# Attention with a softmax that is kept unnormalised for one of eight query blocks, on one core

## What is computed

```python
x  = L0_attn_x                                   # [8, 1024, 512]
xn = layernorm(x)
q, k, v = xn @ Wq.T, xn @ Wk.T, xn @ Wv.T        # 16 heads of 32
attn = softmax(q k^T * 512**-0.5)                # [b, h, s, t]
attn = attn + bias_table[s - t + 1023]           # added after the softmax; the index is clipped at 1022
s = layernorm(attn v) * ln_gamma + ln_beta
h = square(relu(xn @ W_fc.T)); y = h @ W_proj.T  # 2048 hidden
g = silu(mean over 5 steps of the spikes of a leaky integrator driven by y)
return x + s * g
```

## Time and profile before

| | |
|---|---|
| median of three runs | 3528.83 us (3526.05 to 3529.1) |
| span of the profiled execution | 3528.6 us; the page gives no time outside the span |
| feed-forward part, 0 to 1330 us | PE busy 1307.08 us |
| 1500 to 3400 us | PE busy 1856.82 us, ACT 1887.48, DVE 1548.66, POOL 1311.54 of 1900 |
| granted TensorE clock | 1.00 in that stretch, that is 2.4 GHz |

### The profile page before, as it was taken

One profiled execution on the slowest core, in us unless ns is written; L12 is line 12 of the kernel. 1 busy time (PEld: TensorE's weight loads), 2 busy tenths in 40 slices (PEclk: granted clock), 3 DMA queues, 4 the chain that ended last, 5 costly groups with the idle time before them and its releaser, 6 DMA issues.

```text
span 3528.6 us, 55344 instructions
## 1 busy us (share of the span) xinstructions
PE 3421.4 (97%) x19961; PEld 1441.3 (41%) x19964; DVE 2506.6 (71%) x4051; ACT 2624.2 (74%) x3898; POOL 1720.5 (49%) x998
## 2 busy tenths in 40 slices
PE   7999999999999999999999999999999999999996
PEld 3444444444444444433433433433433433433431
DVE  5555555555555555777888888888888888888887
ACT  6433333333333335999999999999999999999997
POOL 0012222111111123899666666666666666666672
PEclk9999999999999999999999999999999999999999
DMA  5122322333222222222322322322322322322322
GB/s 186 57 80 80 104 79 80 101 96 103 80 79 79 81 83 86 83 67 72 121 88 84 95 87 83 96 87 84 96 85 83 98 85 82 100 85 82 100 61 84
DMA packets 238752, 312.35 MB, mean 89 GB/s; under 512 B 96624, under 2 KB 132208, under 8 KB 238480
## 3 DMA queue, kind: packets, MB, share of 16 engines
q1 hardware_dynamic: 238480, 308.82, 28.2%
HBM read 174.65 MB, written 76.61 MB: 71 GB/s over the span
## 4 chain that ended last, share of the span: by engine, by line
ACT 33%; PE 11%; issue 10%; DVE 4%; SPq 1%; DMA 1%; ACTq 0%; POOL 0%; DVEq 0%; POOLq 0%
ACT recurrence_or_probs L1457 17%; ACT s_sb L1464 16%; PE misc L1331 3%; PE acc L1406 3%; PE s_ps L1386 3%; PE s_ps L1372 2%; DVE s_sb L1533 2%; DMA xT<-xnT 1%; SPq L322 1%; DVE gate_or_tokens L1662 0%; PE misc L1313 0%; DVE outT L1553 0%; DVE x_or_queries L1570 0%; DVE gate_or_tokens L1665 0%; PE s_ps L1331 0%
## 5 line engine op out<-in xcount | busy, mean ns | idle before, releaser
L1739 POOL TENSOR_TENSOR recurrence_or_probs<-recurrence_or_probs,toep 128x512 f32<-128x512 f32 (+1 forms) x375 | 1288.5, 3457 | 366.5 <-ACT recurrence_or_probs L1457 366.2
L1533 DVE TENSOR_SCALAR_CACHE_REDUCE s_sb<-s_ps 128x1024 f32<-128x1024 f32 x998 | 1213.7, 1220 | 353.8 <-PE s_ps L1372 325.7
L1464 ACT ACTIVATE s_sb<-s_sb,nmax 128x1024 f32<-128x1024 f32 x998 | 1167.0, 1169 | 9.8 <-DVE s_sb L1533 9.5
L1457 ACT ACTIVATE recurrence_or_probs<-s_ps 128x1024 f32<-128x1024 f32 x1024 | 1060.1, 1036 | 7.7 <-PE s_ps L1386 7.5
L559 PE MATMUL ps_fc<-xnT_part,w_fc 128*128 128x512 f16 x3072 | 707.2, 380 | 4.5 <-DVE w_fc L817 4.5
L574 PE MATMUL ps_y<-w_pr,hid_part 128*128 128x512 f16 x3072 | 706.2, 380 | 3.6 <-issue 2.6
L740 ACT ACTIVATE relu<-ps_fc 128x512 f32<-128x512 f32 x256 | 152.7, 597 | 626.9 <-PE ps_fc L559 626.9
L130 POOL TENSOR_TENSOR recurrence_or_probs<-gate_or_tokens,beta_row 128x512 f32<-128x512 f32 x60 | 89.9, 1499 | 1035.3 <-DVE gate_or_tokens L185 1031.7
L929 DVE TENSOR_TENSOR hid<-relu 128x512 f32<-128x512 f32 x256 | 210.3, 822 | 510.9 <-ACT relu L740 510.9
L1406 PE MATMUL acc<-recurrence_or_probs,val 128*32 128x512 f32 x4096 | 545.2, 604 | 2.2 <-DVE recurrence_or_probs L1649 1.5
L559 PEld LDWEIGHTS ps_fc<-xnT_part,w_fc 128*128 128x128 f16 x3072 | 300.6, 98 | 369.3 <-issue 7.8
(11 more groups left out here) (180 smaller groups left out, 2685.1 us busy)
## 6 DMA issues: line engine op xcount, KB each, us to landing
toep<-table_rows SPq DMA_DIRECT2D x32, 2048.0 KB, 8.3
x_or_queries<-x_or_queries SPq DMA_DIRECT2D x384, 64.0 KB, 2.0
x_or_queries<-in_x SPq DMA_DIRECT2D x16, 1024.0 KB, 10.4
xnT<-xnT_part SPq DMA_DIRECT2D x32, 512.0 KB, 8.5
x_or_gate<-in_x SPq DMA_DIRECT2D x16, 1024.0 KB, 9.2
base<-x_or_gate SPq DMA_DIRECT2D x16, 1024.0 KB, 6.8
xT<-xnT SPq DMA_DIRECT2D x32, 512.0 KB, 9.7
result<-gate_or_tokens SPq DMA_DIRECT2D x64, 256.0 KB, 2.0
```

Source lines behind the costliest of these rows:

```text
L1457: nc.scalar.activation(prob[:, k % PROBS, 2 * second:2 * second + 2, :].rearrange("p j n -> p (j n)"), s_ps[:, item_buffer(pair_item(m)), ...
L1464: nc.scalar.activation(s_sb[:, i % 4, :], s_sb[:, i % 4, :], ACT.Exp, bias=nmax[:, par, j, st:st + 1], scale=-1.0, accum_out=den[:, par, j ...
L1533: nc.vector.tensor_scalar(s_sb[:, i % 4, :], s_ps[:, item_buffer(tile_item(n)), :], -1.0, None, ALU.mult, ALU.min, accum_out=nmax[:, par, ...
L1739: nc.gpsimd.tensor_tensor(tile, tile, toep[:, par, :, at:at + width], ALU.add).then_inc(biased, 1)
```

## The change

Six things change in attention.

1. **The last query block** (`LATE = 7`, queries 896 to 1023) is no longer normalised before the exponential. Its four tiles of a group still give their row maximum (by `tensor_reduce`, with no copy), but `exp_sum` skips them; the logarithm that is subtracted for them stays 0. The order of the tiles (`TILE_ORDER`) puts them at half steps 12, 21, 27 and 2. `s_sb` has three buffers instead of four.
2. **Its denominators**: POOL adds the eight key blocks' exponentials of those 128 queries (`sum_late`, seven additions of 128x512), PE sums them over the keys with a matrix of ones (`late_denominators`, half step 3 of the next slot), and DVE takes the reciprocal and multiplies the output by it.
3. **The bias**: the table now holds differences from its last row, which is zero for the constant part; the constant part is added as the sum of all values of the batch times that row, from sums of tokens that DVE takes in the feed-forward part (`sum_tokens`, two in each chunk) and one set of 48 products in slot 0. `sum_values` of every slot goes. For the last query block PE weighs the bias with the values (`late_bias`, half step 8), and POOL's additions for it go.
4. **The order of the keys** is `KEY_ORDER`, so that wide and narrow additions on POOL alternate.
5. **Weighings come in twos**, in the second half step of every odd step: those of k-3 and k-2.
6. **The projections** are placed anew: the values at half steps 0, 1, 5 and 6, each projection of queries or keys in three parts of four products instead of two of six, and the hand-over of the subtracted rows one half step later.

In the prologue the table is loaded and stored back before the second set of weights is loaded; in the last slot the gate's last tiles are loaded into `xT`.

```diff
+TILE_ORDER = ((0, 0), (0, 1), (0, 2), (0, 3), (1, 0), (1, 1), (0, 7), (1, 2), (1, 3), (2, 0), (2, 1), (2, 2), (2, 3), (3, 0), (3, 1), (1, 7),
...
+LATE = 7
...
-VALUES = {0: (0, 0), 2: (0, 1), 4: (1, 0), 6: (1, 1)}
...
-SUM_VALUES, ROWS_1, ROWS_0, OUT_1, OUT_0 = 8, 10, 27, 28, 30
+VALUES = {0: (0, 0), 1: (0, 1), 5: (1, 0), 6: (1, 1)}
+QUERY_KEYS = {12 + 4 * u + i: (u, i) for u in range(4) for i in range(3)}
+QK_PARTS = 3
+LATE_BIAS = 8
+FAR_VALUES, ROWS_1, ROWS_0, OUT_1, OUT_0 = 4, 10, 28, 29, 30
+KEY_ORDER = ((4, 0, 5, 1, 6, 2, 7, 3), (0, 4, 1, 5, 2, 3, 6, 7))
+COPY_1, COPY_0 = 4, 20
...
+        def weighed_at(b, hg, k):
+
+            ready = (k - WEIGH_LAG, k - WEIGH_LAG + 1) if k % 2 else ()
+            return [(b, hg, i) if i >= 0 else (*before(b, hg), SLOT_STEPS + i) for i in ready]
...
+            def late_denominators(g):
+
+                take_misc()
+                pe.wait_ge(biased, pool_count(g, SLOT_STEPS - 1))
+                pe.wait_ge(ones_made, 1)
+                for j in range(HG):
+                    last = nc.tensor.matmul(misc[j * HD:(j + 1) * HD, :P], ones_col[:], late_sum[:, j, :], start=True, stop=True)
...
+            def late_bias(s):
+
+                take_misc()
+                pe.wait_ge(v_read, s.g * 2 + 2)
+                pe.wait_ge(toep_loaded[s.par], toep_uses(s.b, s.hg) * 16)
+                for j in range(HG):
+                    last = nc.tensor.matmul(misc[j * HD:(j + 1) * HD, :P], val[:, s.par, LATE, j * HD:(j + 1) * HD],
+                                            toep[:, s.par, j, TW - P:], start=True, stop=True)
...
             def exp_sum(G, par, i):
                 n = G * 32 + i
-                j, st = i % 16 // 4, i // 16 * 4 + i % 4
+                j, st = TILE_ORDER[i]
+                if not SUMMED[i]:
+                    return
+                copy = summed_before(n) % COPIES
...
+                if not SUMMED[i]:
+                    nc.vector.tensor_reduce(nmax[:, par, j, st:st + 1], s_ps[:, item_buffer(tile_item(n)), :], AX, ALU.max,
+                                            negate=True).then_inc(max_done, 1)
+                    return
...
+                nc.vector.reciprocal(late_scale[:], misc[:, :P]).then_inc(den_read, 1)
+                nc.vector.tensor_scalar(outT[:, 1, :late.start], acc[:, :late.start], from_far, None, ALU.add)
+                dve.wait_ge(den_read, g + 1)
+                nc.vector.tensor_tensor(outT[:, 1, late], acc[:, late], late_scale[:], ALU.mult).then_inc(acc_read, 1)
+                dve.wait_ge(acc_read, g * 2 + 2)
+                nc.vector.tensor_tensor(outT[:, 1, late], outT[:, 1, late], late_out[:], ALU.add).then_inc(out_made, 1)
...
+            def sum_late(b, hg, k):
+
+                g, late = b * HG + hg, slice(LATE * P - 512, 512)
+                if k < 9:
+                    return
+                if k == 9:
+                    wait(pool, den_ps, g)
+                pool.wait_ge(p_done, g * 32 + k * 2 + 2)
+                if k > 9:
+                    pool.wait_ge(biased, pool_count(g, k - 1))
+                before_it = late_sum[:] if k > 9 else prob[:, 8 % PROBS, :, late]
+                nc.gpsimd.tensor_tensor(late_sum[:], before_it, prob[:, k % PROBS, :, late], ALU.add).then_inc(biased, 1)
```

290 lines of the change are left out of this document (190 added, 100 removed).

## The result

The changed kernel took 3653.43 us (median of 4 runs, 3652.68 to 3658.92), the kernel before 3527.94 (3526.05 to 3529.1): a ratio of 1.0359, 95% interval 1.0344 to 1.0374. The profiled execution has a span of 3657.1 us, 128.5 more than before. Forecast was slower, by 34; it is slower by 126. The sign is right, the size and the range are not.

What follows compares the result with a forecast made beforehand. ACT and PE, both nearly full, were taken as tied by the ring of three. Ordinary slots +17, GpSimd in slots 1 and 2 +12 and ends +4 make 33 on 3528.6: 3562 us, range 3503 to 3602.

Steps and rivals of the forecast that it cites:

- Room of 1.9 us, the ring of three: Between a tile and the next pair, PE has 1.9 us for other work before ACT waits; 5.2 of waits a slot.
- The transposes' wait of 0.95: At the subtracted rows' hand-over, PE's first transpose waits 0.95 us for DVE's cast.
- ACT 65.7 to 61.4: In an ordinary slot, leaving out four sums lowers ACT's work from 65.7 to 61.4 us.
- Between 0 and 0.7, and I take 0.4: Ordinary slot: waits for DVE add 0.4 us, giving 67.0 against 66.4 measured before.
- as they were: DVE's bursts at half steps 19 to 23 were taken as unchanged, some falling where ACT waits anyway.
- R3: Rival: GpSimd's sums stretch four two-operand DVE operations at half steps 19 to 23; 42 us more, 3604; chance 0.14.
- The reciprocal, "0.3 taken, costs nothing up to about 1 us": DVE's reciprocal at half step 4: between 0.2 and 1.1 us, 0.3 taken, free up to about 1.
- GpSimd in slots 1 and 2, +12: GpSimd's added work doesn't fit in slots 1 and 2: some 5 to 6 us each, +12; 0 to 16 possible.
- Ends, +4: Later prologue weights, 48 small products in slot 0 and steps behind the last weighing: +4 us in all.
- R1: Rival: engines' sums decide, the ring is no bound; slot 63.3, time 3458 us, chance 0.12.
- R2: Rival: row hand-over is free, transposes don't wait for DVE; slot 66.0, time 3522 us, chance 0.20.
- has a light stretch: PE has little work at half step 4, so DVE's reciprocal there was said to cost nothing.

Runs made afterwards that it cites:

- e6: Changed kernel with only the first of GpSimd's late sums per slot and the second half's key blocks in order 0 to 7: 3600.9 us.
- e15: Kernel before plus GpSimd's seven sums over the late block, weighing waiting for them, result unused: 3577.42 us.
- e8: Changed kernel with DVE's 128x128 reciprocal replaced by a copy of the same tile: 3636.38 us.
- e1: Changed kernel with only the first of GpSimd's seven late sums kept in each slot: 3627.81 us.
- e9: Changed kernel with the two steps that finish a token row working on 8 of its 512 columns: 3601.75 us.
- e10: Changed kernel with the four tiles without a sum moved to half steps 8, 12, 24 and 28: 3615.64 us.
- e4: Changed kernel with exponential and sum on ACT again for the late query block's four tiles, sums unused: 3671.51 us.
- e11: Changed kernel with second-half key blocks in order and GpSimd doing the gate product and base addition of token rows: 3626.91 us.
- e14: Changed kernel with new tile and key order, GpSimd finishing rows, late block at half steps 8 and 9 with PSUM operands, gate spread evenly: 3618.91 us.
- e2: Changed kernel with one weighing at every odd half step; also moves the copies and late denominators two half steps later: 3695.14 us.
- e12: Changed kernel with late denominators, reciprocal and the two steps behind it moved from half steps 3 and 4 to 8 and 9: 3813.95 us.
- e17: Changed kernel with the score products of half steps 8 to 10 issued twice: 3649.72 us, ratio 1.0346.

## Why the prediction was right and wrong

- **Room of 1.9 us, the ring of three:** right as a mechanism, its total in part by luck. It gave 5.2 of waits a slot where 4.2 and 0.9 of small ones were measured, 0.34 at half steps 0 and 1 (0.34), 1.33 at 3 (1.27), and 0.46 and 0.48 at 13 and 15 (0.40 and 0.47). At 22 and 23 it had 1.12, measured 0.6, and at 28 to 31 1.14, measured 0.9. In their place stand the 0.70 of half step 12 behind the clock's dips, which the prediction didn't have. The transposes' wait of 0.95 was 0.64, since PE came there later.
- **ACT 65.7 to 61.4:** right (65.8 and 61.7).
- **"Between 0 and 0.7, and I take 0.4" for DVE's bursts:** the step that failed. It is 2.9. The 2.5 a slot between 0.4 and 2.9 are 71 of the 95 us by which the span misses 3562; the rest is 8 of the remaining terms of the ordinary slots, 5 of slots 1 and 2, and 12 of the ends. I took the burst of half steps 19 to 23 "as they were". It wasn't: the key order and the late sums put GpSimd's additions there (0.98 of the waits go with them, e6; 0.69 are also in the kernel before with the sums, e15). This is R3, which had 14%, though not with its operations: the four that it names took 0.94 and 0.98 us on average instead of 0.75, 0.8 a slot together, while Newton's first two steps, which it didn't name, went from 0.17 to 1.0 and 1.2, and with the next ones add 1.1 a slot. The place of the reciprocal adds 0.41 (e8). 1.55 are left, where the kernel before had 0.43, and no step of the prediction had them.
- **The reciprocal, "0.3 taken, costs nothing up to about 1 us":** failed twice. It took 0.96, inside the bounds but at the end not chosen, and it stands with the statistics in the half steps that have no room; 0.41 a slot of waits for DVE (e8).
- **GpSimd in slots 1 and 2, +12:** 16.6, just above the upper bound named, with PE waiting for GpSimd as it said. e15 has 16.8 from the sums alone, e1 gives 12.3 back.
- **Ends, +4:** 4.7 before slot 1, but 11.5 in the last slot and the tail, which had been given 1.5. In the last slot GpSimd's wide additions of the bias stand beside DVE's two-operand steps (4.93 and 4.36 us above). The late sums aren't the cause there, since with one sum left the last slot is still 6.6 longer than before (50.8 against 44.2); with DVE's work on the rows cut short it is 45.4 (e9).
- **R1** (engines' sums decide) is excluded by e10 and e4: the ring decides. **R2** (hand-over free) would have needed no wait at the transposes; 0.86 was there.

What stays open: with hardly any addition beside it DVE still makes ACT wait 1.96 a slot (e6), of which 0.41 are at half step 5, where the late block stands, and 0.96 at half step 23. The kernel before had 0.43 in all and 0.01 at half step 23, with the same finishing steps. Nearly half of this one hangs on the skipped sum of half step 21: with that tile summed (e4) or moved (e10) it is 0.56 instead of 1.02. Single weighings (2.59 of waits for DVE) and all sums kept (2.81) did not bring the whole back. e9, e11 and e14 show that it goes with DVE's work in those half steps (1.39, 1.36, 0.59); why the same work cost less before isn't shown.

## What to carry to other kernels

Before a change puts work on GpSimd, list DVE's steps in the same stretch and look where their operands are: one with two operands in SBUF, however short, can cost the length of GpSimd's instruction, and of all that follow it without a break. Moving such a step by a few half steps is enough to bring it there (e2, e12). Work taken off the busiest engine pays only what the ring behind it lets through: here 4.1 us of ACT's work bought 0.7. And a half step in which another engine "has a light stretch" is not free: price a step there by whether its own consumer has room.

## What the runs showed of the hardware

- DVE 128x128 products: 4353 ns with two SBUF operands beside GpSimd's 4.56 us additions, 281 and 291 with one in PSUM.
- The wait doesn't end with one GpSimd instruction: beside three GpSimd additions without a break between them (4.5, 1.3 and 4.5 us) a 128x128 sum with two SBUF operands took 7.12 us (e11), and a step on 4 columns with one tensor operand 8.48 (e14, slot 4).
- A scalar step on 4 columns of SBUF, with one tensor operand, also takes 1.0 to 1.2 us beside GpSimd's 1.27 us additions, against 0.16 to 0.17 with GpSimd idle.
- A reciprocal of 128x128 takes 0.96 us, 3.4 times a product of that shape (0.28).
- Two windows of 2 us with PE busy for 1.12 and 1.30 of them are followed by 3.4 us at a granted clock of 0.50, the lower level; this happened in 11 of 27 slots, and each time ACT waited 1.5 to 1.6 us. With the idling filled no 2 us window of these slots was below 1.00 (e17).
